# Deferred PSUM copies, a reordered layer norm pipeline, a carried head tail and an early output-weight load in a differential-attention and FFN kernel on eight cores

## The chip, the cores and the metric

The kernel runs on the 8 cores of one Trainium2 chip, with no traffic between them. Core c works on batch element c // 2, and of its 2048 rows on every second block of 128 (8 blocks, 1024 rows). The metric is the device time of the slowest core in microseconds (us), the median over runs.

## The reference, cut to what matters

```python
xn = _layernorm(x)                              # x: (4, 2048, 2048)
s = attn(xn)
g = silu(ffn(xn))
return x + s * g

def attn(x):                                    # 8 heads, two maps of width 128 each
    q1, q2 = split(x @ Wq); k1, k2 = split(x @ Wk)
    vcat = concat(split(x @ Wv))                # width 256
    attn1 = softmax(causal(q1 @ k1.T * scale)) @ vcat
    attn2 = softmax(causal(q2 @ k2.T * scale)) @ vcat
    a = attn1 - lambda_full * attn2
    a = a * rsqrt(mean(a * a) + EPS) * subln_weight * (1.0 - LAMBDA_INIT)
    return heads_joined(a) @ Wo

def ffn(x):                                     # INTER = 5632
    hdn = silu((x @ gate_w.T) * gate_s) * ((x @ up_w.T) * up_s)
    return (hdn @ down_w.T) * down_s
```

## The kernel before

All instruction streams are written out by hand in program order, one list for each engine, and tied by counting semaphores (`wait(engine, semaphore, value)`). Each engine runs its list strictly in order, so the place of an instruction in the emission order decides what stands behind it. Three counters matter: `sT` for TensorE (PE), `sV` for VectorE (DVE), `sS` for ScalarE (ACT). PSUM is split in `psA` and `psB`. The first 1024 columns of `psA` are two slots of 512 that `take_slot` hands out in turn, to projection rounds and to score groups alike; before a slot is written again, PE waits for what emptied it (`slot_guard`).

**Stage 1, layer norm and the projections of head 0 (lines 337 to 480).** A loop over 24 tiles of 128 rows: 16 key/value tiles (all rows of the batch element), then 8 of the core's own rows. For a tile t: `ln_stageA` squares it on ACT (L369) and sums it on DVE (L372); `ln_var` and `ln_rstd` make the inverse deviation (DVE L385 and L389, then Ln and Exp on ACT, L394 and L397); `ln_affine` normalises it on DVE (L404, L408); `ln_tp` transposes it on PE, 16 float32 transposes in four groups (L201, `psB<-ident,xn_nat`), each group copied out by ACT (L434). `h0_rounds` then runs head 0's projection rounds on what is there: a V round for each key/value tile (16 matmuls of 256 columns), two K rounds with every fourth (16 matmuls of 512 columns each), two Q rounds with every fourth own tile. ACT copies each round out right after it (L317, L321, L325). In iteration t the order is rstd(t-1), affine(t-1), transposes(t-1) with their copies, square and sum of t, variance of t, rounds of t-1. The x tiles rotate through three buffers, loaded by the SP queue.

**Stage 2, attention, a loop over 8 heads (lines 483 to 658).** For heads 1 to 7 the 4 Q rounds and the K and V rounds of chunks 0 and 1 (12 rounds) run ahead of the head's tiles; the 12 rounds of chunks 2 and 3 are `pending` and are put one by one between scores and values, one for each map in tiles 0 to 5. DVE copies each round out (L316, L320, L324). For tile tl (0 to 7) and each map beta: score groups of up to 4 blocks, the last group first (PE, then the exponential on ACT, L605; only the last group gets the mask multiply on DVE, L615), a pending round, then the values product into an accumulator that alternates by tl. There are 1 group in tiles 0 and 1, 2 in tiles 2 and 3, 3 in 4 and 5, 4 in 6 and 7. After both maps of tile tl, `emit_combine(tl - 1)` is emitted: ten small DVE steps (L526 to L543), Ln and Exp on ACT (L546, L548), a last DVE step (L553). `emit_atp` transposes its result on PE later (L201, `psB<-ident,a_out`), and ACT copies it (L572). At the end of a head its last combine and transposes are emitted before the next head's Q rounds. GpSimd loads the next head's weights.

**Stage 3, the FFN** in six chunks. The change doesn't touch it. Its result stays in `out_accT` in SBUF.

**Stage 4, gate and output (lines 776 to 865).** 32 groups of 4 transposes of `out_accT` go through two slots of `psB`, each followed by a Silu on ACT into `g_sb` (L795). Then GpSimd loads `wo` into `wo_sb`, four pieces of 2 MB as stored; `wo_sb` lies on the same bytes as `out_accT`, piece i exactly on the four `out_accT` columns blocks of g4 = i. The output product needs all four pieces for its first result; DVE multiplies by the gate and adds x (L851, L853), the SP queue stores.

Of the kernel before, what the change touches and what calls it, by code (L numbers as in the profile page):

```python
# [7 lines left out]
AF = mybir.ActivationFunctionType  # L8
ALU = mybir.AluOpType
AX = mybir.AxisListType.X  # L10
# [27 lines left out]
def build_nc(cfg):  # L38
# [237 lines left out]
    slot_guard = [[], []]  # L276

    def take_slot():
# [6 lines left out]
    def emit_proj_round(h, kind, aa, bb, extra_s_wait=0, evac="vector"):  # L285
# [40 lines left out]
        if evac == "vector":  # L326
            wait("vector", sT, last_c)
            c = sV.bump()
            E("vector", lambda v, fn=fnv, hh=sV.h: fn(v).then_inc(hh, 1))
            slot_guard[i] = [(sV, c)]  # L330
            return (sV, c)
        else:
            wait("scalar", sT, last_c)
            c = sS.bump()
            E("scalar", lambda s, fn=fns, hh=sS.h: fn(s).then_inc(hh, 1))
            slot_guard[i] = [(sS, c)]
            return (sS, c)
# [99 lines left out]

    def h0_rounds(tt):
        ev = sS.n
        if tt < TS:  # L440
            emit_proj_round(0, "v", tt, 0, extra_s_wait=ev, evac="scalar")
            if tt % 4 == 3:
                sc = tt // 4
                emit_proj_round(0, "k", 0, sc, extra_s_wait=ev, evac="scalar")
                emit_proj_round(0, "k", 1, sc, extra_s_wait=ev, evac="scalar")
        else:
            if (tt - TS) % 4 == 3:
                qc = (tt - TS) // 4
                emit_proj_round(0, "q", 0, qc, extra_s_wait=ev, evac="scalar")
                emit_proj_round(0, "q", 1, qc, extra_s_wait=ev, evac="scalar")  # L450

    c_xnT_full = None
    for t in range(NT):
        if t >= 1:
            ln_rstd(t - 1)
            ln_affine(t - 1)
            if t + 2 < NT:
                emit_xdma(t + 2)
            ln_tp(t - 1)
            if t - 1 == TS - 1:  # L460
                c_xnT_full = sS.n
        ln_stageA(t)
        ln_var(t)
        if t >= 1:
            h0_rounds(t - 1)
# [5 lines left out]
    h0_rounds(NT - 1)  # L471
    c_xnT_own = sS.n
# [8 lines left out]

    c_proj_evacs_s0 = sS.n
    for h in range(H):
# [8 lines left out]
        def emit_round(spec):  # L492
            c, kind, aa, bb = spec
            ev = emit_proj_round(h, kind, aa, bb)
            if kind == "v" and aa == 4 * c + 3:
                c_chunk_ev[c] = ev
            return ev

        if h > 0:
            first = True  # L500
            for j in range(2):
                for qc in range(NQC):
                    emit_proj_round(h, "q", j, qc,
                                    extra_s_wait=(c_xnT_own if first else 0))
                    first = False
            for c in range(min(2, NSC)):
                for spec in chunk_rounds(c):
                    emit_round(spec)
            for c in range(2, NSC):
                pending += chunk_rounds(c)  # L510
# [6 lines left out]

        def emit_combine(tl):
            avslot = tl % 2
            avbase = psA[:, 1024:2048] if avslot == 0 else psB[:, 0:1024]  # L520
            av1 = avbase[:, 0:512]
            av2 = avbase[:, 512:1024]
            if h == 0 and tl == 0:
                wait("vector", sLAM, c_lam)
                wait("vector", sV, cv_w2)
            cv = V(lambda v, av1=av1: v.reciprocal(sm_rr1[:, 0:1], av1[:, 256:257]))  # L526
            cv = V(lambda v, av2=av2: v.reciprocal(sm_rr2[:, 0:1], av2[:, 256:257]))
            wait("vector", sV, cv)
            cv = V(lambda v: v.tensor_mul(sm_rr2l[:, 0:1], sm_rr2[:, 0:1],
                                          lamneg[:, 0:1]))  # L530
            wait("vector", sV, cv)
            cv = V(lambda v, av1=av1: v.tensor_scalar(  # L532
                t_comb[:, :], av1[:, 0:256], sm_rr1[:, 0:1], None, ALU.mult))
            wait("vector", sV, cv)
            c_av_free[avslot] = V(lambda v, av2=av2: v.scalar_tensor_tensor(  # L535
                t2buf[:, :], av2[:, 0:256], sm_rr2l[:, 0:1], t_comb[:, :],
                ALU.mult, ALU.add))
            wait("vector", sV, c_av_free[avslot])
            cv = V(lambda v: v.tensor_mul(t_comb[:, :], t2buf[:, :], t2buf[:, :]))  # L539
            wait("vector", sV, cv)  # L540
            cv = V(lambda v: v.reduce_sum(sm_ms[:, 0:1], t_comb[:, :], axis=AX))  # L541
            wait("vector", sV, cv)
            cv_ms = V(lambda v: v.tensor_scalar(  # L543
                sm_ms[:, 0:1], sm_ms[:, 0:1], 1.0 / 256, 1e-5, ALU.mult, ALU.add))
            wait("scalar", sV, cv_ms)
            cs = SC(lambda s: s.activation(sm_rst[:, 0:1], sm_ms[:, 0:1], AF.Ln))  # L546
            wait("scalar", sS, cs)
            c_rstd = SC(lambda s: s.activation(  # L548
                sm_rst[:, 0:1], sm_rst[:, 0:1], AF.Exp, scale=-0.5))
            wait("vector", sS, c_rstd)  # L550
            wait("vector", sT, c_atp_slot[tl % 2])
            ao = a_out[:, (tl % 2) * 256:(tl % 2) * 256 + 256]
            c_aout = V(lambda v, ao=ao: v.scalar_tensor_tensor(  # L553
                ao, t2buf[:, :], sm_rst[:, 0:1], W2[:, :],
                ALU.mult, ALU.mult))
            return c_aout

        def emit_atp(tl, c_aout):
            atp = tl % 2
            ao = a_out[:, atp * 256:atp * 256 + 256]  # L560
            tp = psB[:, 1024 + atp * 512:1024 + atp * 512 + 512]
            wait("tensor", sV, c_aout)
            wait("tensor", sS, c_atp_free[atp])
            for j in range(2):
                TP(tp[:, j * 128:(j + 1) * 128], ao[:, j * 128:(j + 1) * 128],
                   inc=(j == 1))
            c_atp_slot[atp] = sT.n
            wait("scalar", sT, c_atp_slot[atp])
            dst = aT.rearrange("p (at s) -> p at s", s=OWN)[
                :, 2 * h:2 * h + 2, tl * 128:(tl + 1) * 128]  # L570
            c_atp_free[atp] = sS.bump()
            E("scalar", lambda s, dst=dst, tp=tp, hh=sS.h: s.copy(  # L572
                dst, tp.rearrange("p (j c) -> p j c", c=128)[:, 0:2, :]
            ).then_inc(hh, 1))

        pend_atp = []
        for tl in range(TO):
# [4 lines left out]
            while pending and pending[0][0] <= tl // 2:  # L582
                emit_round(pending.pop(0))
# [59 lines left out]
            if len(pend_atp) >= 2:  # L643
                emit_atp(*pend_atp.pop(0))
            if tl > 0:
                ca = emit_combine(tl - 1)
                pend_atp.append((tl - 1, ca))
        if len(pend_atp) >= 2:
            emit_atp(*pend_atp.pop(0))
        ca = emit_combine(TO - 1)  # L650
        pend_atp.append((TO - 1, ca))
        while pend_atp:
            emit_atp(*pend_atp.pop(0))
# [124 lines left out]

    gb_slot_free = [0, 0]
    wait("tensor", sV, c_ffn_done)  # L780
    for tl in range(TO):
        for g4 in range(KD // 4):
            gslot = g4 % 2
# [3 lines left out]
            for kk in range(4):  # L787
# [9 lines left out]
                AF.Silu).then_inc(hh, 1))  # L797
    c_g_done = sS.n

    wo_r = wo.rearrange("(kt p) n -> p kt n", p=128)  # L800
    c_wo = []
    for c4 in range(KD // 4):
        if c4 == 0:
            wait("gpsimd", sS, c_g_done)
        c_wo.append(dma("gpsimd", sWO[c4],
                        wo_sb.rearrange("p (kt n) -> p kt n", n=D)[:, c4 * 4:(c4 + 1) * 4, :],
                        wo_r[:, c4 * 4:(c4 + 1) * 4, :]))
# [182 lines left out]
```

## Time and profile before

| | us |
|---|---|
| median of 3 runs (2566.83, 2572.0, 2770.03) | 2572.0 |
| the profiled execution | 2565.12 |
| its span on the slowest core, core 3 | 2563.6 |
| spans of the eight cores | 2531.9 to 2563.6 |
| PE / DVE / ACT busy on core 3 | 2052.6 / 655.1 / 401.6 |

Three lines of the page show the span of core 3 in 40 equal slices of 64 us, each digit the busy share in tenths (PEclk: the clock granted to TensorE in tenths of full speed):

```profile
PE   2655547879787878787787998998998998999388
ACT  2333333030302121121213000000000000000200
PEclk9766668989998989899899999999999999999689
```

Slices 1 to 6 are stage 1, 7 to 22 attention, 23 to 37 the FFN, the last three stage 4. PE is the engine that is busy most, but not in stage 1 (about 5 tenths, at a clock of 0.6) nor in the third slice from the end. The page's largest waits of PE are these (engine, line, waited for: us in total, times, longest):

```profile
PE psA L194 <- ACT p_buf L605: 148.1, 98, 3.9
PE psB L201 <- DVE xn_nat L408: 123.8, 24, 39.9
PE psA L194 <- ACT xn_nat L369: 48.5, 17, 3.1
PE psA L194 <- DMA wo_sb<-wo: 47.9, 4, 23.1
PE psB L201 <- DVE a_out L553: 29.9, 8, 3.7
```

The first is in attention, the next two in stage 1, the fourth in stage 4, the last at the ends of the heads.

### The profile page before, as it was taken

The numbers are of one execution on the slowest core, as the hardware profiler recorded it, in microseconds if no ns is written. First come the engines' busy times: TensorE is split into PE (matmuls) and PEld (weight loads), VectorE is DVE, ScalarE is ACT, GpSimd is POOL, SyncE is SP. The second block draws the span as 40 slices with busy tenths as digits, with TensorE's granted clock in tenths as the row PEclk, the third lists the DMA queues.
The fourth block names the chain that finished last, engine by engine and source line by source line (L and its number), as shares of the span: only waits on it lengthen the run. The fifth ranks groups of instructions, "written<-read, shape, count | busy, mean of one in ns | idle before, by whom it ended". The sixth has DMA issues, their size and how long they took to land.

```text
span 2563.6 us, 28997 instructions; the slowest of 8 cores (2531.9 to 2563.6 us)
## 1 busy us (share of the span) xinstructions
PE 2052.6 (80%) x11264; PEld 1130.6 (44%) x11264; DVE 655.1 (26%) x1282; ACT 401.6 (16%) x812; POOL 136.3 (5%) x126
## 2 busy tenths in 40 slices
PE   2655547879787878787787998998998998999388
PEld 1433324545555555555455443443443443444234
DVE  2322323232323232333323022021131130123033
ACT  2333333030302121121213000000000000000200
POOL 0000000000000000000000110100101101100000
PEclk9766668989998989899899999999999999999689
DMA  7221231121212112121107956747638729731643
GB/s 135 75 74 66 82 65 18 17 34 17 34 17 34 17 18 33 17 34 17 17 1 87 93 52 84 71 43 99 66 33 114 69 34 107 72 50 17 134 129 132
DMA packets 246058, 147.88 MB, mean 58 GB/s; under 512 B 183587, under 2 KB 232997, under 8 KB 240678
## 3 DMA queue, kind: packets, MB, share of 16 engines
q0 software_dynamic: 239008, 102.77, 34.1%
q1 hardware_dynamic: 6918, 43.25, 4.8%
q8 instruction: 95, 1.56, 0.2%
q14 instruction: 37, 0.30, 0.0%
HBM read 240.38 MB, written 8.39 MB: 97 GB/s over the span
## 4 chain that ended last, share of the span: by engine, by line
PE 74%; DVE 8%; DMA 7%; ACT 6%; issue 5%; DVEq 0%; POOL 0%; ACTq 0%; SPq 0%; POOLq 0%
PE psA L194 52%; PE psB L194 18%; PE psB L201 4%; DMA up_sb<-up_wT 3%; ACT p_buf L605 2%; DMA wo_sb<-wo 2%; ACT xn_nat L369 2%; DVE xn_nat L408 1%; DVE t_comb L532 1%; DVE t2buf L535 1%; DVE t_comb L539 1%; DVE sm_ms L541 1%; DVE vbuf L324 1%; DVE kT L320 1%; ACT sm_rst L546 1%
## 5 line engine op out<-in xcount | busy, mean ns | idle before, releaser
L194 PE MATMUL psA<-wv_sb,xnT_full 128*128 128x256 bf16 x2048 | 282.7, 303 | 77.4 <-ACT xn_nat L369 45.6
L194 PEld LDWEIGHTS psA<-wv_sb,xnT_full 128*128 128x128 bf16 x2048 | 215.4, 107 | 136.3 <-issue 91.6
L194 PE MATMUL psA<-xnT_full,wk_sb 128*128 128x512 bf16 x1024 | 243.3, 396 | 38.0 <-ACT p_buf L605 29.8
L605 ACT ACTIVATE p_buf<-psA 128x512 bf16<-128x512 f32 (+1 forms) x320 | 165.4, 550 | 563.9 <-PE psA L194 555.4
L194 PE MATMUL psA<-xnT_own,gate_sb 128*128 128x512 bf16 x704 | 166.2, 397 | 38.1 <-DMA up_sb<-up_wT 38.1
L201 PE MATMUL psB<-ident,xn_nat 128*128 128x128 f32 x384 | 87.5, 406 | 125.0 <-DVE xn_nat L408 123.8
L194 PE MATMUL psA<-qT,kT 128*128 128x128 bf16 x1152 | 109.3, 229 | 94.9 <-ACT p_buf L605 90.1
L194 PEld LDWEIGHTS psA<-xnT_full,wk_sb 128*128 128x128 bf16 x1024 | 102.0, 101 | 165.5 <-issue 61.7
L194 PE MATMUL psA<-hdn,down_sb 128*128 128x512 bf16 x704 | 159.7, 379 | 11.2 <-DVE hdn L737 11.0
L194 PE MATMUL psB<-hdn,down_sb 128*128 128x512 bf16 x704 | 159.8, 379 | 0.0
L194 PE MATMUL psA<-xnT_own,up_sb 128*128 128x512 bf16 x704 | 155.5, 379 | 0.0
L194 PE MATMUL psB<-xnT_own,gate_sb 128*128 128x512 bf16 x704 | 155.5, 379 | 0.0
L194 PE MATMUL psB<-xnT_own,up_sb 128*128 128x512 bf16 x704 | 155.5, 379 | 0.0
L194 PE MATMUL psA<-wo_sb,aT 128*128 128x512 bf16 x512 | 116.0, 390 | 47.9 <-DMA wo_sb<-wo 47.9
L194 PEld LDWEIGHTS psA<-qT,kT 128*128 128x128 bf16 x1152 | 83.3, 103 | 116.0 <-issue 110.9
L201 PEld LDWEIGHTS psB<-ident,xn_nat 128*128 128x128 f32 x384 | 68.3, 210 | 145.1 <-issue 142.3
L194 PE MATMUL psA<-xnT_own,wq_sb 128*128 128x512 bf16 x512 | 126.2, 412 | 3.9 <-ACT xn_nat L369 2.8
L194 PEld LDWEIGHTS psA<-xnT_own,gate_sb 128*128 128x128 bf16 x704 | 71.0, 101 | 130.5 <-issue 54.9
L727 ACT ACTIVATE silu_g<-psA,gate_sc 128x1024 f32<-128x1024 f32 x22 | 24.5, 1114 | 601.2 <-PE psA L194 601.2
L737 DVE SCALAR_TENSOR_TENSOR hdn<-psA,up_sc,silu_g 128x1024 bf16<-128x1024 f32 x22 | 28.2, 1284 | 328.0 <-PE psA L194 328.0
L194 PEld LDWEIGHTS psA<-hdn,down_sb 128*128 128x128 bf16 x704 | 67.9, 98 | 96.6 <-issue 16.5
L194 PEld LDWEIGHTS psA<-xnT_own,up_sb 128*128 128x128 bf16 x704 | 68.9, 98 | 83.0
(83 smaller groups left out, 1677.6 us busy)
## 6 DMA issues: line engine op xcount, KB each, us to landing
gate_sb<-gate_wT POOLq DMA_DIRECT2D x44, 512.0 KB, 7.7
up_sb<-up_wT POOLq DMA_DIRECT2D x44, 512.0 KB, 9.4
down_sb<-down_wT POOLq DMA_DIRECT2D x5, 4096.0 KB, 30.9
x_stage<-x_kv SPq DMA_DIRECT2D x16, 1024.0 KB, 5.6
wq_sb<-wq POOLq DMA_DIRECT2D x8, 1024.0 KB, 9.4
wk_sb<-wk POOLq DMA_DIRECT2D x8, 1024.0 KB, 9.4
wv_sb<-wv POOLq DMA_DIRECT2D x8, 1024.0 KB, 9.2
x_stage<-x_own SPq DMA_DIRECT2D x8, 1024.0 KB, 4.9
```

Source lines behind the costliest of these rows:

```text
L194: tn.matmul(o, l, r, start=st, stop=sp, skip_group_check=True)))
L201: tn.transpose(o, i_, ident[:, :])))
L320: fnv = lambda e, d=d_, ps=ps: e.tensor_copy(d, ps)
L324: fnv = lambda e, d=d_, ps=ps: e.tensor_copy(d, ps[:, 0:256])
L369: cs_sq[t] = SC(lambda s, xs=xs, xn=xn, t=t: s.activation(xn, xs, AF.Square, accum_out=st_ssq[:, t:t + 1]))
L408: c_ln_aff[t] = V(lambda v, xs=xs, xn=xn, t=t: v.tensor_scalar(xn, xs, st_rstd[:, t:t + 1], st_nmr[:, t:t + 1], ALU.mult, ALU.add))
L532: cv = V(lambda v, av1=av1: v.tensor_scalar(t_comb[:, :], av1[:, 0:256], sm_rr1[:, 0:1], None, ALU.mult))
L535: c_av_free[avslot] = V(lambda v, av2=av2: v.scalar_tensor_tensor(t2buf[:, :], av2[:, 0:256], sm_rr2l[:, 0:1], t_comb[:, :], ALU.mult, ALU ...
L539: cv = V(lambda v: v.tensor_mul(t_comb[:, :], t2buf[:, :], t2buf[:, :]))
L541: cv = V(lambda v: v.reduce_sum(sm_ms[:, 0:1], t_comb[:, :], axis=AX))
L605: s.activation(pb[:, g * 512:g * 512 + w], ps[:, 0:w], AF.Exp).then_inc(hh, 1))
L737: v.scalar_tensor_tensor(hdn[:, itl * OWN:(itl + 1) * OWN], gps[:, OWN:2 * OWN], up_sc[:, it:it + 1], silu_g[:, :], ALU.mult, ALU.mult).th ...
```

## The change

Four edits, all in the order of emission; no instruction is added or taken away.

1. **Stage 1, order.** Square, sum and variance of tile t are emitted ahead of the transposes of tile t-1 and their copies. The rounds of t-1 then wait for those copies and no longer for the square of t.
2. **Deferred copies.** A round's copy out of PSUM is no longer emitted behind its matmuls, but when its slot is next taken (`slot_pending`, `drain_slot` in `take_slot`). This holds for head 0's rounds in stage 1 (on ACT) and for the 12 pending rounds of each later head (on DVE); the 16 rounds ahead of a head's tiles keep their copy behind them (`defer=False`).
3. **Head tail.** The last combine of a head and its outstanding transposes are carried over and emitted after the next head's 16 leading rounds (after the last head, as before). `emit_combine` and `emit_atp` are moved out of the loop unchanged but for a head argument.
4. **Stage 4.** The loop over gate groups runs g4 outside and tl inside, and each piece of `wo` is issued after its g4 is through, instead of all after the last.

```diff
     def take_slot():
         i = PS_["i"]
         PS_["i"] ^= 1
+        drain_slot(i)
         for sem, cnt in slot_guard[i]:
             wait("tensor", sem, cnt)
         return i, psA[:, i * 512:i * 512 + 512]
...
+        if defer:
+            return i, do_evac
+        return do_evac()
...
+    def h0_emit(kind, aa, bb, ev):
+        i, th = emit_proj_round(0, kind, aa, bb, extra_s_wait=ev, evac="scalar",
+                                defer=True)
+        slot_pending[i] = th
...
             ln_affine(t - 1)
             if t + 2 < NT:
                 emit_xdma(t + 2)
+        ln_stageA(t)
+        ln_var(t)
+        if t >= 1:
             ln_tp(t - 1)
             if t - 1 == TS - 1:
                 c_xnT_full = sS.n
-        ln_stageA(t)
-        ln_var(t)
-        if t >= 1:
             h0_rounds(t - 1)
...
+            def fin(th=th, c=c, kind=kind, aa=aa):
+                ev = th()
+                if kind == "v" and aa == 4 * c + 3:
+                    c_chunk_ev[c] = ev
+            if defer:
+                slot_pending[i] = fin
+            else:
+                fin()
...
+        if carry is not None:
+            hp, patp = carry
+            if len(patp) >= 2:
+                emit_atp(hp, *patp.pop(0))
+            ca = emit_combine(hp, TO - 1)
+            patp.append((TO - 1, ca))
+            while patp:
+                emit_atp(hp, *patp.pop(0))
+            carry = None
...
             while pending and pending[0][0] <= tl // 2:
-                emit_round(pending.pop(0))
+                emit_round(pending.pop(0), defer=False)
+            if h > 0 and c_chunk_ev[tl // 2] is None:
+                drain_all_slots()
...
-        if len(pend_atp) >= 2:
-            emit_atp(*pend_atp.pop(0))
-        ca = emit_combine(TO - 1)
-        pend_atp.append((TO - 1, ca))
-        while pend_atp:
-            emit_atp(*pend_atp.pop(0))
+        drain_all_slots()
+        carry = (h, pend_atp)
...
-    for tl in range(TO):
-        for g4 in range(KD // 4):
-            gslot = g4 % 2
+    for g4 in range(KD // 4):
+        for tl in range(TO):
+            gslot = (g4 * TO + tl) % 2
...
+        wait("gpsimd", sS, gb_slot_free[(g4 * TO + TO - 1) % 2])
+        c_wo[g4] = dma("gpsimd", sWO[g4],
+                       wo_sb.rearrange("p (kt n) -> p kt n", n=D)[:, g4 * 4:(g4 + 1) * 4, :],
+                       wo_r[:, g4 * 4:(g4 + 1) * 4, :])
```

## Rows read from the trace of the kernel before

**Rows 1.** Windows by stage, core 3: stretch, length, busy (instructions) by engine, clock, DMA, GB/s

```profile
39.95:276.40 236.45, 143.66 (x640) 94.36 (x641) 69.22 (x113) 83.32 (x152) 0.00 (x0) 0.70 0.20 71
276.40:365.20 88.80, 46.06 (x193) 29.30 (x194) 30.24 (x50) 36.97 (x64) 0.43 (x1) 0.65 0.17 60
435.90:1394.17 958.27, 764.75 (x5266) 501.51 (x5264) 296.84 (x812) 182.09 (x448) 26.00 (x23) 0.92 0.19 24
2369.30:2393.80 24.50, 19.62 (x128) 13.41 (x128) 0.14 (x1) 18.92 (x32) 0.00 (x0) 1.00 0.00 1
2393.80:2446.50 52.70, 5.61 (x13) 1.35 (x14) 0.00 (x0) 0.00 (x0) 2.98 (x4) 0.53 0.97 199
```

**Rows 2.** Timeline of one key/value tile: start, us, engine, work, [idle before <-releaser]

```profile
183.42 3.85 PE L201 MATMUL psB<-ident,xn_nat 128*128 128x128 f32 x16 [3.03 <-DVE xn_nat L408]
...
187.84 1.91 ACT L369 ACTIVATE xn_nat<-x_stage 128x2048 f32<-128x2048 f32 x1
...
190.09 3.57 PE L194 MATMUL psA<-wv_sb,xnT_full 128*128 128x256 bf16 x16 [2.83 <-ACT xn_nat L369]
...
194.03 0.21 ACT L394 ACTIVATE st_rstd<-st_t 128x1 f32<-128x1 f32 x1
...
194.90 1.35 DVE L408 TENSOR_SCALAR xn_nat<-x_stage,st_rstd,st_nmr 128x2048 f32<-128x2048 f32 x1
...
196.50 3.85 PE L201 MATMUL psB<-ident,xn_nat 128*128 128x128 f32 x16 [2.84 <-DVE xn_nat L408]
```

**Rows 3.** Timeline: two K rounds, an own tile, an own tile with Q rounds

```profile
206.54 8.13 PE L194 MATMUL psA<-xnT_full,wk_sb 128*128 128x512 bf16 x32
...
295.14 3.85 PE L201 MATMUL psB<-ident,xn_nat 128*128 128x128 f32 x16 [5.73 <-DVE xn_nat L408]
...
304.72 3.47 PE L201 MATMUL psB<-ident,xn_nat 128*128 128x128 f32 x16 [5.73 <-DVE xn_nat L408]
...
322.84 1.06 PE L201 MATMUL psB<-ident,xn_nat 128*128 128x128 f32 x8 [3.05 <-DVE xn_nat L408]
323.56 1.07 ACT L434 CAST xnT_own<-psB 128x512 bf16<-128x512 f32 x2 [2.69 <-PE psB L201]
```

**Rows 4.** Windows of 4 us in head 0's attention, columns as in rows 1

```profile
396.00:400.00 4.00, 2.95 (x16) 2.20 (x16) 2.61 (x10) 1.25 (x6) 0.00 (x0) 0.52 0.00 2
...
404.00:408.00 4.00, 2.09 (x23) 1.68 (x23) 2.45 (x7) 2.02 (x6) 0.00 (x0) 1.00 0.00 0
```

**Rows 5.** Timeline of tiles 1 and 2 of a head with pending rounds

```profile
763.20 0.69 DVE L320 CAST kT<-psA 128x512 bf16<-128x512 f32 x1 [3.46 <-PE psA L194]
...
766.05 0.42 DVE L324 CAST vbuf<-psA 128x256 bf16<-128x256 f32 x1 [1.29 <-PE psA L194]
766.22 0.39 PE L194 MATMUL psA<-qT,kT 128*128 128x128 bf16 x4
766.62 1.91 PE L194 MATMUL psA<-wv_sb,xnT_full 128*128 128x256 bf16 x16
766.70 0.60 ACT L605 ACTIVATE p_buf<-psA 128x512 bf16<-128x512 f32 x1 [2.48 <-PE psA L194]
767.40 0.42 DVE L615 TENSOR_TENSOR p_buf<-p_buf,masks 128x512 bf16<-128x512 bf16 x1 [0.93 <-ACT p_buf L605]
...
768.97 0.16 DVE L526 RECIPROCAL sm_rr<-psA 128x1 f32<-128x1 f32 x1
...
772.05 0.20 ACT L546 ACTIVATE sm_rst<-sm_ms 128x1 f32<-128x1 f32 x1 [4.75 <-DVE sm_ms L543]
...
772.97 3.57 PE L194 MATMUL psA<-wv_sb,xnT_full 128*128 128x256 bf16 x16 [3.38 <-ACT p_buf L605]
```

**Rows 6.** Timeline of the end of a head and the next head's start

```profile
839.18 2.03 PE L194 MATMUL psB<-vbuf,p_buf 128*128 128x257 bf16 x16
...
847.39 0.66 PE L201 MATMUL psB<-ident,a_out 128*128 128x128 f32 x2 [3.74 <-DVE a_out L553]
847.84 2.72 PE L194 MATMUL psA<-xnT_own,wq_sb 128*128 128x512 bf16 x6
```

More of the change, by code:

```diff
@@ L276, in build_nc, with drain_slot, drain_all_slots @@
     slot_guard = [[], []]
+    slot_pending = [None, None]
+    def drain_slot(i):
+        if slot_pending[i] is not None:
+            th = slot_pending[i]
+            slot_pending[i] = None
+            th()
+    def drain_all_slots():
+        drain_slot(0)
+        drain_slot(1)
     def take_slot():
@@ L325, in emit_proj_round, with do_evac @@
             fns = lambda e, d=d_, ps=ps: e.copy(d, ps[:, 0:256])
[L326 to L337, printed above, removed]
+        def do_evac():
+            if evac == "vector":
+                wait("vector", sT, last_c)
+                c = sV.bump()
+                E("vector", lambda v, fn=fnv, hh=sV.h: fn(v).then_inc(hh, 1))
+                slot_guard[i] = [(sV, c)]
+                return (sV, c)
+            else:
+                wait("scalar", sT, last_c)
+                c = sS.bump()
+                E("scalar", lambda s, fn=fns, hh=sS.h: fn(s).then_inc(hh, 1))
+                slot_guard[i] = [(sS, c)]
+                return (sS, c)
+        if defer:
+            return i, do_evac
+        return do_evac()
     NT = TS + TO
@@ L448, in h0_rounds @@
                 qc = (tt - TS) // 4
[L449 to L450 removed]
+                h0_emit("q", 0, qc, ev)
+                h0_emit("q", 1, qc, ev)
     c_xnT_full = None
@@ L480, in build_nc, with emit_combine @@
         vones.rearrange("p (t c) -> p t c", c=1)).then_inc(hh, 1))
+    def emit_combine(h, tl):
+        avslot = tl % 2
+        avbase = psA[:, 1024:2048] if avslot == 0 else psB[:, 0:1024]
+        av1 = avbase[:, 0:512]
+        av2 = avbase[:, 512:1024]
+        if h == 0 and tl == 0:
+            wait("vector", sLAM, c_lam)
+            wait("vector", sV, cv_w2)
+        cv = V(lambda v, av1=av1: v.reciprocal(sm_rr1[:, 0:1], av1[:, 256:257]))
+        cv = V(lambda v, av2=av2: v.reciprocal(sm_rr2[:, 0:1], av2[:, 256:257]))
+        wait("vector", sV, cv)
+        cv = V(lambda v: v.tensor_mul(sm_rr2l[:, 0:1], sm_rr2[:, 0:1],
+                                      lamneg[:, 0:1]))
+        wait("vector", sV, cv)
+        cv = V(lambda v, av1=av1: v.tensor_scalar(
+            t_comb[:, :], av1[:, 0:256], sm_rr1[:, 0:1], None, ALU.mult))
+        wait("vector", sV, cv)
+        c_av_free[avslot] = V(lambda v, av2=av2: v.scalar_tensor_tensor(
+            t2buf[:, :], av2[:, 0:256], sm_rr2l[:, 0:1], t_comb[:, :],
+            ALU.mult, ALU.add))
+        wait("vector", sV, c_av_free[avslot])
+        cv = V(lambda v: v.tensor_mul(t_comb[:, :], t2buf[:, :], t2buf[:, :]))
+        wait("vector", sV, cv)
+        cv = V(lambda v: v.reduce_sum(sm_ms[:, 0:1], t_comb[:, :], axis=AX))
+        wait("vector", sV, cv)
+        cv_ms = V(lambda v: v.tensor_scalar(
+            sm_ms[:, 0:1], sm_ms[:, 0:1], 1.0 / 256, 1e-5, ALU.mult, ALU.add))
+        wait("scalar", sV, cv_ms)
+        cs = SC(lambda s: s.activation(sm_rst[:, 0:1], sm_ms[:, 0:1], AF.Ln))
+        wait("scalar", sS, cs)
+        c_rstd = SC(lambda s: s.activation(
+            sm_rst[:, 0:1], sm_rst[:, 0:1], AF.Exp, scale=-0.5))
+        wait("vector", sS, c_rstd)
+        wait("vector", sT, c_atp_slot[tl % 2])
+        ao = a_out[:, (tl % 2) * 256:(tl % 2) * 256 + 256]
+        c_aout = V(lambda v, ao=ao: v.scalar_tensor_tensor(
+            ao, t2buf[:, :], sm_rst[:, 0:1], W2[:, :],
+            ALU.mult, ALU.mult))
+        return c_aout
@@ new lines, in emit_atp @@
+    def emit_atp(h, tl, c_aout):
+        atp = tl % 2
+        ao = a_out[:, atp * 256:atp * 256 + 256]
+        tp = psB[:, 1024 + atp * 512:1024 + atp * 512 + 512]
+        wait("tensor", sV, c_aout)
+        wait("tensor", sS, c_atp_free[atp])
+        for j in range(2):
+            TP(tp[:, j * 128:(j + 1) * 128], ao[:, j * 128:(j + 1) * 128],
+               inc=(j == 1))
+        c_atp_slot[atp] = sT.n
+        wait("scalar", sT, c_atp_slot[atp])
+        dst = aT.rearrange("p (at s) -> p at s", s=OWN)[
+            :, 2 * h:2 * h + 2, tl * 128:(tl + 1) * 128]
+        c_atp_free[atp] = sS.bump()
+        E("scalar", lambda s, dst=dst, tp=tp, hh=sS.h: s.copy(
+            dst, tp.rearrange("p (j c) -> p j c", c=128)[:, 0:2, :]
+        ).then_inc(hh, 1))
@@ L490, in chunk_rounds, with emit_round @@
             return r
-        def emit_round(spec):
+        def emit_round(spec, defer=True):
             c, kind, aa, bb = spec
[L494 to L497, printed above, removed]
+            i, th = emit_proj_round(h, kind, aa, bb, defer=True)
+            def fin(th=th, c=c, kind=kind, aa=aa):
[4 more added lines that the diff above has]
+                slot_pending[i] = fin
+            else:
+                fin()
         if h > 0:
@@ L516, in build_nc @@
         w_prefetched = False
[L518 to L574, printed above, removed]
+        if carry is not None:
[6 more added lines that the diff above has]
+                emit_atp(hp, *patp.pop(0))
+            carry = None
```

33 lines of the change are left out of this document (18 added, 15 removed).

## The prediction

> **What bounds the kernel now.** I read the spans and clocks of the cores first (undisturbed, all at about 0.90), then the page's slices, then windows cut at the stage borders, then the list of waits to see which stage each big wait of PE lies in, and last the timeline of one unit of each stage that the diff touches. The windows [rows 1] say where there is anything to win. The 16 key/value tiles of stage 1 take 236.45 us with PE busy for 143.66 at a granted clock of 0.70; the 8 own tiles 88.80 with PE busy for 46.06. The seven heads with pending rounds take 958.27 at 0.92, 136.9 each. The gate transposes take 24.50, and the load of `wo` behind them 52.70, with PE nearly idle and the DMA engines at 0.97. The FFN, untouched, is dense.
>
> No engine bounds stage 1; a chain does. In one tile [rows 2] the reader sees it walk over three engines: transposes at 183.42, the square of the next tile at 187.84 behind the last copy, the V round at 190.09, which waited 2.83 for that square, Ln at 194.03 behind the round's copy, the affine at 194.90, next transposes at 196.50. That is 13.08 us for 7.4 us of matmuls, and PE idles twice for 2.8 us.
>
> **Edit 1 and 2 in stage 1.** The square (1.91 on ACT) now runs beside the affine and the first transposes, and Ln(t) no longer stands behind the copy of V round t-1, but behind that of a round two takes older, done long before. The cycle left is: transposes and their four copies, 4.42 (187.84 - 183.42); then the old copy, about 0.3; then two branches in parallel. On PE the V round starts at about 4.9 and keeps PE 3.4 (3.57 less the drain of the last matmul). On ACT and DVE, Ln to next transposes is 2.47 (196.50 - 194.03), ready at 7.2. PE is last: 8.3 us a tile at the low clock of 1.2 GHz, in place of 13.08. Every fourth tile adds two K rounds, 8.13 [rows 3]: they now run on behind the V round, with the affine hidden under them. Four tiles: 4 x 8.3 + 8.1 = 41.3, all 16: 165, a gain of 71.
>
> At 2.4 GHz the transposes are copy-bound: 8 of them in 1.06, two copies in 1.07 from 0.72 after the start [rows 3]; with two slots the four copies end at about 3.1. Add 0.3 and 2.47: 5.9 a tile, the ACT and DVE branch being last (the V round, 1.91 [rows 5], ends at 5.5). K rounds are four times a V round's column work, 7.0, of which 6.6 shows. Four tiles 30.2, all 121, a gain of 115.
>
> Which clock? Before, it is mostly low, and each tile has idle gaps of 2.8 and 3.0 us. Afterwards the longest gap I can construct is 1.2 to 1.3 us (last transpose to V round), and at the low clock PE would be busy 7 of 8.3 us. In head 0's attention the clock rose from 0.52 to 1.00 around a stretch busy 2.95 of 4.00, and stayed at 1.00 in one busy 2.09 of 4.00 [rows 4], close to the 3.5 of 5.9 I expect here at the high level. So I take three quarters of the stage at the high level: 132 us, a gain of 104. Range 71 to 115.
>
> The Trainium skill (TensorE: Matmul & The Clock Gate, Part 4: PE-mode transpose) says the full clock doesn't engage for transposes, which don't count as busy in the same way; half of PE's work here is transposes. By that the gain would be the 71 of the low level. The trace speaks against it: 24.50 us of nothing but such transposes ran at 1.00 [rows 1]. It shows the level being held, not reached, so the low case stays a rival.
>
> Own tiles: 9.58 (5.73 + 3.85 [rows 3]) becomes 4.42 + 2.47 = 6.9 since the square leaves the chain; six of them save 16. The tile with Q rounds took 18.12 (304.72 to 322.84); now 4.9 + 8.7 = 13.6, saving 4.5. Together 21. The last tile keeps its chain. The x loads are issued by SP behind the same affine as before and are needed two periods later, 12 us at the least; the DMA share of 0.20 would at most double. DVE has 4.3 us of work in a tile (69.22 over 16), ACT 5.2 (83.32 over 16) [rows 1], both under 5.9.
>
> **Edit 2 in attention.** This one costs. Drained at the next take of its slot, a pending round's copy goes into DVE's list behind the mask of the score group emitted just before, and PE's very next take waits for it. In rows 5: round r3 starts at 766.62, 0.40 after its scores (766.22), since the previous copy (766.05) was long in. Now DVE would do the mask first: exponential 766.70 to 767.30, mask 767.40 to 767.82, copy 0.42, so r3 at 768.4: +1.8. Behind PE's wait stand the round and the values product; nothing else can run. A head has seven such places (second map of tile 0, both of tile 1, second maps of 2 to 5). With a narrow exponential, or where the round waited for an exponential anyway, it is 1.0 to 1.1; with a K copy (0.69 [rows 5]) or a third group 1.5. Sum of the seven: 10.1; bounds 7 and 12.6.
>
> The other five places, the first maps of tiles 2 to 6, gain. There the combine of an earlier tile stood on DVE behind the copy of the round just finished (it starts at 768.97), its Ln came 3.08 later, and the exponentials of the next tile stood behind that Ln on ACT, so PE waited 3.38 for r4. Now the combine starts as r3 starts, 2.3 us earlier against r3, but scores' second group then waits for exponential, L553, mask and copy. From r3 to r4 I get 5.3 in place of 6.35 (772.97 - 766.62). The five give 0.6 to 1.45 each, 4.9 in all; bounds 3 and 7. Net +5.2 a head, +36 for seven; bounds 0 and +67.
>
> **Edit 3.** Before, PE has nothing from the end of the last values product (841.2) to the first Q round (847.84) but four transposes: 6.6 us [rows 6]. The carried combine is emitted after the sixteen rounds with DVE's copies ahead of it, and the transposes that need it still stand ahead of the next scores on PE. So the stall isn't hidden, it moves: copy 0.42, combine 4.2 (3.08 to Ln [rows 5], Ln, Exp and L553), transposes 0.6: 5.2. What is gained is the end of the combine before it, 1.4 a head, 10 in all. Bounds: nothing, and 2.5 a head.
>
> **Edit 4.** Piece 0 is issued a quarter into the 24.50 us, 18.4 earlier. The pieces are issued every 6.1 us while one takes 13.2 of the 52.70, so the chain of four slides by the full 18.4; the x loads are issued as before and share the engines as before. Below bound 12, if the new order slows transposes or copies.
>
> **Sum**, against the profiled execution's own 2565.1: -104 - 21 + 36 - 10 - 18 = -117, which gives 2448. The median of the runs shown is 7 us above it, the lowest 2 above; I leave the forecast at 2448. About 2% (51 us) is what a measurement of this kernel can tell from no change.
>
> **Rivals.** (a) *Stage 1 stays at 1.2 GHz*, by the rule on transposes or because short gaps are enough: +33, 2481. The mean clock of the stage decides, which before is 0.70. 17%. (b) *The deferred copies cost their upper bound*, 9.6 a head in place of 5.2: +31, 2479. For it: the waits of PE for DVE and ACT in series at every slot; against: all durations are from rows. 12%. (c) *Slower, by the clock in attention.* The new 1.5 to 2 us stalls come between those of 2.5 to 3 us that stay, and the heads run at 0.92 on the strength of their density. If the twelve rounds, scores and values of the loop (an estimate of 51 us of matmul time a head at the full clock: 8 V rounds at 1.75, 4 K rounds at 3.5, and 144 blocks at 0.11 for values and 0.055 for scores, scaled by columns from r3's 1.91 [rows 5]) went to the low level, the price would be up to 45 a head, 315 in all, 2763. It cancels the gain from 17 us a head, when over a third of this work runs low. Against it: rows 4, where stalls of the same kind leave the clock at 1.00. 4% for slower by over 2%, 5% for a part of it that ends within 2%. (d) *The reverse*: shorter longest stalls keep the heads at the high level where they now fall (r4 takes 3.57 at 772.97 where r3 took 1.91): -3 a head, 2425. 12%. The forecast itself has 50%.
>
> The range takes in (a), (b), (d) and the high bound of stage 1: 2405 to 2500, with some 10% on either side, more above. Faster by over 2% means under 2521: 0.91 (the forecast, a, b and d); same 0.05; slower 0.04.
>
> **What would show it.** Right: first Q round of head 1 some 125 us earlier; tiles of about 6 us with the V round released by an ACT copy and clock near 1.0 up to the own tiles, where it falls; in the heads, PE waiting 1 to 2 us for DVE copies (L320, L324) inside tiles, and for L553 in front of a head's first scores rather than its Q rounds; heads of about 140 us; `wo` waits of about 30. Wrong: a clock under 0.7 in stage 1, tiles of 8 us or more, heads over 150 or under 136.

## The result: 4.9% faster

| | before | after |
|---|---|---|
| median of 10 runs | 2653.63 us | 2443.87 us |
| lowest | 2566.83 us | 2437.53 us |
| profiled execution, its span | 2565.12, 2563.6 us | 2437.53, 2436.0 us |
| ratio, 95% interval | | 0.9507 [0.9491, 0.9523] |

Five of the ten runs of before and three of the ten of the changed kernel fell in a slower state that this chip shows in some executions of any kernel, which lifts the medians; the ratio and all times below leave such runs out (2567 to 2572 is left, against 2438 to 2450). The forecast was 2448 and a ratio of 0.952.

The windows of the changed kernel, cut at the same borders as [rows 1] (core 1, its slowest; length, busy time and instructions of PE, PEld, DVE, ACT, POOL, granted clock, DMA share, GB/s): key/value tiles, own tiles, heads 1 to 7, gate transposes, the wait for `wo`.

```profile
40.60:167.00 126.40, 98.01 (x654) 68.22 (x655) 71.82 (x117) 78.86 (x152) 0.00 (x0) 1.00 0.44 142
167.00:230.40 63.40, 41.17 (x180) 26.38 (x179) 27.63 (x45) 33.94 (x62) 0.40 (x1) 0.73 0.21 67
...
293.60:1284.20 990.60, 759.09 (x5273) 499.67 (x5271) 293.65 (x824) 183.79 (x455) 26.00 (x23) 0.93 0.18 23
...
2258.30:2282.40 24.10, 19.61 (x128) 13.39 (x128) 0.00 (x0) 18.90 (x32) 2.23 (x3) 1.00 0.63 103
2282.40:2319.10 36.70, 4.76 (x13) 1.23 (x14) 0.00 (x0) 0.03 (x1) 0.74 (x1) 0.55 1.00 219
```

Against [rows 1], the 236.45 us of the key/value tiles became 126.40, and the clock 1.00 in place of 0.70; the own tiles went from 88.80 to 63.40; the seven heads from 958.27 to 990.60, longer; the wait for `wo` from 52.70 to 36.70. By stage, on the slowest core of each kernel (stage 1 from the first transpose to the first score, attention from there to the first gate matmul, the FFN from there to the first gate transpose): stage 1 325.3 to 189.8, attention 1028.9 to 1053.8, FFN 975.5 to 974.1, everything after the gate transposes 170.9 to 154.5. That is -135.5, +24.9, -1.4 and -16.4; with a first transpose 0.7 us later, it gives the 127.6 between the spans.

One key/value tile of the changed kernel (timeline, columns as in [rows 2]):

```profile
58.65 0.22 ACT L410 ACTIVATE st_rstd<-st_t 128x1 f32<-128x1 f32 x1
58.90 1.91 PE L194 MATMUL psA<-wv_sb,xnT_full 128*128 128x256 bf16 x16 [1.39 <-ACT st_rstd L410]
...
59.06 1.90 ACT L385 ACTIVATE xn_nat<-x_stage 128x2048 f32<-128x2048 f32 x1
...
59.52 1.35 DVE L424 TENSOR_SCALAR xn_nat<-x_stage,st_rstd,st_nmr 128x2048 f32<-128x2048 f32 x1
...
61.13 1.06 PE L201 MATMUL psB<-ident,xn_nat 128*128 128x128 f32 x8 [0.32 <-ACT xn_nat L385]
...
62.58 1.12 PE L201 MATMUL psB<-ident,xn_nat 128*128 128x128 f32 x8 [0.39 <-ACT xnT_full L450]
...
64.79 1.91 PE L194 MATMUL psA<-wv_sb,xnT_full 128*128 128x256 bf16 x16 [1.10 <-ACT vbuf L337]
```

From V round to V round it is 5.89 us where [rows 2] has 13.08. Ln starts before the V round and no longer behind its copy; the square and the affine run beside the round; PE's gaps are 1.10, 0.32 and 0.39, and its matmuls run at nearly twice the speed of [rows 2] (1.91 for the V round against 3.57).

### The profile page after: what moved, and what is told of

It is laid out like the page before. It is cut to its first block, busy times and chain, and to the rows that moved or that the text cites. A ratio compares the mean times of both kernels' runs of the same rounds, so it can differ in the third digit from the quotient of the medians.

```text
span 2436.0 us, 29000 instructions; the slowest of 8 cores (2387.9 to 2436.0 us)
## 1 busy us (share of the span) xinstructions
PE 1997.2 (82%) x11264; PEld 1100.3 (45%) x11264; DVE 648.4 (27%) x1282; ACT 396.2 (16%) x812; POOL 136.3 (6%) x126
## 4 chain that ended last, share of the span: by engine, by line
PE 74%; DVE 7%; DMA 6%; ACT 6%; issue 5%; DVEq 0%; ACTq 0%; POOL 0%; SPq 0%; POOLq 0%
PE psA L194 52%; PE psB L194 19%; DMA up_sb<-up_wT 3%; ACT p_buf L646 3%; PE psB L201 3%; DMA wo_sb<-wo 1%; DVE vbuf L336 1%; DVE kT L332 1%; DVE st_sum L388 1%; ACT xn_nat L385 1%; DVE t_comb L518 1%; DVE t2buf L521 1%; DMA x_stage<-x_kv 1%; DVE a_out L539 1%; DVE p_buf L656 1%
## 5 line engine op out<-in xcount | busy, mean ns | idle before, releaser
L194 PE MATMUL psA<-wv_sb,xnT_full 128*128 128x256 bf16 x2048 | 267.3, 293 | 60.8 <-ACT p_buf L646 16.5
L194 PEld LDWEIGHTS psA<-wv_sb,xnT_full 128*128 128x128 bf16 x2048 | 208.9, 104 | 108.9 <-issue 71.0
L194 PE MATMUL psA<-xnT_full,wk_sb 128*128 128x512 bf16 x1024 | 248.4, 402 | 11.4 <-DVE kT L332 11.4
L656 DVE TENSOR_TENSOR p_buf<-p_buf,masks 128x512 bf16<-128x512 bf16 (+1 forms) x128 | 45.8, 358 | 367.8 <-ACT p_buf L646 362.1
L201 PE MATMUL psB<-ident,xn_nat 128*128 128x128 f32 x384 | 64.2, 321 | 69.0 <-DVE xn_nat L424 44.2
L194 PE MATMUL psA<-xnT_own,wq_sb 128*128 128x512 bf16 x512 | 114.0, 384 | 2.6 <-ACT qT L329 1.3
L194 PEld LDWEIGHTS psB<-xnT_own,up_sb 128*128 128x128 bf16 x704 | 68.9, 98 | 83.0
```

Source lines behind the costliest of these rows:

```text
L194: tn.matmul(o, l, r, start=st, stop=sp, skip_group_check=True)))
L201: tn.transpose(o, i_, ident[:, :])))
L656: v.tensor_mul(pb[:, g * 512:g * 512 + w], pb[:, g * 512:g * 512 + w], masks[:, tl * 512:tl * 512 + w]).then_inc(hh, 1))
```

## The experiments

Four kernels make one part of the change each, on the kernel before, with what the part needs of `slot_pending` and its draining. The stage lengths are medians of the eight cores of the profiled execution; for the kernel before they are 324.6 (stage 1), 1026.0 (attention) and 171.0 (after the gate transposes), for the changed kernel 189.4, 1048.8 and 152.2.

| kernel | stage 1 | attention | after the gate | time |
|---|---|---|---|---|
| stage 1 alone | 188.9 | 1025.7 | 170.9 | 2438 to 2452, ratio 0.9477 [0.9413, 0.954] |
| deferred copies in the heads alone | 323.8 | 1067.6 | 171.1 | 2614 to 2630, ratio 1.0165 [1.0108, 1.0223] |
| carried tail alone | 322.9 | 1016.0 | 170.7 | 2570.69, one |
| early `wo` alone | 325.1 | 1025.8 | 154.2 | 2559 to 2573, ratio 0.9935 [0.9896, 0.9975] |

### Stage 1 alone

```diff
+        ln_stageA(t)                     # ahead of ln_tp(t - 1)
+        ln_var(t)
...
+        slot_pending[i] = th             # head 0's copies, drained at the next take
```

> The kernel before with edits 1 and 2 in stage 1 alone; copies in the heads, head tail and wo load as before. Theory (stage 1 is a chain over three engines, and its parts add to the others): stage 1 takes 190 us in place of 325, key/value tiles at a clock of 1.00; total 135 lower, about 2434 against 2569 for the kernel before. Rival (the copies left behind their rounds in the heads, or the later start of the weight loads, take some of it back): a gain under 120, above 2449.

Stage 1 is 135.7 us shorter and nothing else moved, 1025.7 in attention against 1026.0. The theory holds: this part alone gives as much as the whole change, 2438 to 2452 against 2438 to 2450, and by stages somewhat more, 135.7 us against the 127.6 between the spans.

### Deferred copies in the heads alone

```diff
-                    emit_round(pending.pop(0))
+                    emit_round(pending.pop(0), defer=True)
```

> The kernel before with only the copies of the 12 pending rounds of each later head deferred. Theory of the prediction: seven places lose 10.1 us, five gain 4.9, net +5.2 a head, +36 in all, about 2605. Rival A (the carried head tail really hides its stall, and the deferral costs all of what the tail gave): attention as a whole came out 25 longer, so the deferral would be +65, 2634. Rival B (the clock in the heads falls with the added stalls): over +60 with a mean clock in the heads under 0.90. Rival C (the deferral is free, and the tail costs the 25): 2569.

Attention is 41.6 us longer, 5.9 a head where 5.2 was forecast, so rivals A (65) and C (nothing) fall. Over heads 1 to 7 the granted clock was 0.926 to 0.930 by core, against 0.916 to 0.918 for the kernel before: it didn't fall, and rival B falls too.

### The carried tail alone

```diff
+        carry = (h, pend_atp)            # combine and transposes after the next 16 rounds
```

> The kernel before with only the last combine and transposes of a head carried behind the next head's sixteen leading rounds. Theory: the stall of about 5 us is moved in front of the next head's first scores and only the end of the combine before it is won, 1.4 to 2.5 us a head, 10 to 17 in all, 2552 to 2559. Rival (the stall is hidden): 5 us or more a head, 35 to 45 in all, 2524 to 2534. Rival (it costs, since the clock falls in front of the scores and a K round in place of the Q rounds): 2575 or more.

Attention is 10.0 us shorter, the lower end of the theory, and no more. The total can't decide here: there is one time to compare, 2570.69, and the kernel before, run beside it, took 2572 to 2598. The length of attention does, 1012.5 to 1019.3 by core against 1026.0 to 1029.5.

### The early load of `wo` alone

```diff
-    for tl in range(TO):
-        for g4 in range(KD // 4):
+    for g4 in range(KD // 4):
+        for tl in range(TO):
...
+        c_wo[g4] = dma("gpsimd", sWO[g4], ...)    # after each g4
```

> The kernel before with only the order of the gate groups turned and each piece of wo issued after its quarter. Theory: 16 us less, as between the two traces (52.7 to 36.7 from the last gate transpose to the last wait for wo), 2553. Rival (the earlier pieces only crowd the x loads and the first stores): under 8, 2561 or more.

The part after the gate transposes is 16.8 us shorter, as in the changed kernel. The waits of its output product (timeline of the changed kernel) are 15.03, 7.70 and 8.93 where the kernel before had four, 47.9 in all:

```profile
2298.73 1.87 PE L194 MATMUL psA<-wo_sb,aT 128*128 128x512 bf16 x4 [15.03 <-DMA wo_sb<-wo]
2308.30 1.86 PE L194 MATMUL psA<-wo_sb,aT 128*128 128x512 bf16 x4 [7.70 <-DMA wo_sb<-wo]
2319.09 11.16 PE L194 MATMUL psA<-wo_sb,aT 128*128 128x512 bf16 x41 [8.93 <-DMA wo_sb<-wo]
```

The DMA engines were at 0.63 over the gate transposes and at 1.00 in the 36.70 us behind them: the load is still bound by the transfer, it only starts earlier.

### Each half of the edit in stage 1

The first keeps each copy behind its round and only moves square, sum and variance up; the second only defers the copies.

```diff
+        ln_stageA(t)                     # first kernel
+        ln_var(t)
```

> The kernel before with the square, sum and variance ahead of the transposes in stage 1, but each copy still behind its round. Theory: the square leaves the chain, Ln still stands behind the copy of the V round; a key/value tile is transposes and copies 4.4, V round 3.5, copy 0.4, Ln to transposes 2.5, 10.8 us in place of 13.1 at the low clock; own tiles 6.9 as with both. Gain 16 x 2.3 + 8 x 2.7 = 55 to 60, 2512. If the clock rises as it did with both, tiles of 8.0 and a gain near 100, 2470. Rival (either half alone does it all): 2434.

```diff
+        slot_pending[i] = th             # second kernel
```

> The kernel before with the copies of head 0's rounds deferred in stage 1, but the square still between the transposes' copies and the rounds. Theory: Ln no longer waits for the V round, but the round waits for the square; a key/value tile is transposes and copies 4.4, square 2.1 and its latency, V round 3.4, 10.2 us in place of 13.1 at the low clock; own tiles keep their 9.6 since the square stays in their chain, but for the one with Q rounds (-3). Gain 16 x 2.9 + 3 = 45 to 50, 2521. If the clock rises, tiles of 8.4 and a gain near 80, 2489. Rival (the two edits are additive and this one holds the larger part): 80 or more at a clock as before.

Only stage 1 is read from these two. It took 263.4 and 263.0 (medians, all cores within 261.4 to 264.4): 61 us less for either half, 123 for the two added up, 135.7 together. Both were forecast low, at 55 to 60 and 45 to 50. Their timelines on PE, the order alone first, then the deferral alone:

```profile
183.44 3.39 PE L208 MATMUL psB<-ident,xn_nat 128*128 128x128 f32 x16 [3.05 <-ACT xn_nat L392]
187.75 3.39 PE L201 MATMUL psA<-wv_sb,xnT_full 128*128 128x256 bf16 x16 [0.93 <-ACT xnT_full L457]
193.98 3.62 PE L208 MATMUL psB<-ident,xn_nat 128*128 128x128 f32 x16 [2.83 <-ACT xn_nat L392]
```

```profile
181.59 3.36 PE L208 MATMUL psB<-ident,xn_nat 128*128 128x128 f32 x16
188.15 3.57 PE L201 MATMUL psA<-wv_sb,xnT_full 128*128 128x256 bf16 x16 [3.20 <-ACT kT L340]
191.52 3.36 PE L208 MATMUL psB<-ident,xn_nat 128*128 128x128 f32 x16
```

Each half closes one of the two gaps of [rows 2] and leaves the other: 0.93 and 2.83 in the first, none and 3.20 in the second. The tiles shown take 10.5 and 9.9 us. With one gap of 3 us left, the granted clock over the key/value tiles was 0.77 to 0.81 on all cores; with none it was 1.00. Some 13 us of the 135.7 exist only with both halves, 10 of them in the key/value tiles (43 and 55 less for the halves, 108 together, medians from the first transpose to the end of the last K round). That the clock accounts for them is likely, but no run separates it from the chain.

### Transposes twice, a question on the clock

```diff
-            for kt in kts:
+            for kt in (kts * 2 if t >= TS else kts):     # own tiles only
                 TP(ps[...], xn[:, kt * 128:(kt + 1) * 128], ...)
```

> The changed kernel with each transpose of the 8 own tiles of stage 1 issued twice, same result; a question on the clock alone. In the changed kernel these tiles hold only transposes and idle gaps of 3.0 us and run at 0.50 but for what the K and Q rounds leave behind. Theory (transposes are activity as any matmul): with nearly no gaps the clock goes from 0.50 to 1.00 inside the own tiles and stays there, and the stage gets little longer although its transposes are doubled, 63 to at most 70 us. Rival, by the Trainium skill (TensorE: Matmul & The Clock Gate, Part 4: PE-mode transpose), where the full clock doesn't engage for transposes: 0.50 throughout, tiles of about 10.3 us (transposes 6.9 + the rest of 3.5), the stage near 90.

In the changed kernel the own tiles hold one idle gap of 3.04 us each. Between the K rounds and the Q rounds they run at the low clock (16 transposes in 3.85):

```profile
170.47 3.85 PE L201 MATMUL psB<-ident,xn_nat 128*128 128x128 f32 x16 [3.04 <-ACT xn_nat L385]
177.35 3.85 PE L201 MATMUL psB<-ident,xn_nat 128*128 128x128 f32 x16 [3.04 <-ACT xn_nat L385]
```

Behind the first Q rounds the level went to and fro on core 1 (on core 6 it stayed low), and rose there too after a stretch of nothing but transposes:

```profile
203.80:207.20 3.40, 3.27 (x15) 2.82 (x16) 2.70 (x5) 1.41 (x4) 0.00 (x0) 0.50 0.00 0
207.20:210.60 3.40, 0.36 (x3) 0.15 (x2) 1.75 (x3) 3.18 (x6) 0.00 (x0) 1.00 0.00 0
```

With each transpose doubled, on core 0, first two tiles of the timeline, then windows of 4 us around them:

```profile
203.85 5.35 PE L208 MATMUL psB<-ident,xn_nat 128*128 128x128 f32 x32 [3.04 <-ACT xn_nat L392]
212.25 3.83 PE L208 MATMUL psB<-ident,xn_nat 128*128 128x128 f32 x32 [3.04 <-ACT xn_nat L392]
```

```profile
204.00:208.00 4.00, 4.00 (x23) 4.00 (x23) 2.42 (x5) 1.17 (x2) 0.00 (x0) 0.57 0.00 0
208.00:212.00 4.00, 1.20 (x12) 0.96 (x9) 1.51 (x3) 3.20 (x6) 0.00 (x0) 1.00 0.00 0
212.00:216.00 4.00, 3.75 (x32) 3.46 (x32) 2.82 (x5) 1.92 (x5) 0.00 (x0) 1.00 0.00 0
```

The clock went from 1.2 to 2.4 GHz inside a stretch that holds nothing but transposes, and 32 then took what 16 had taken. The rule of the Trainium skill that I weighed in the prediction (TensorE: Matmul & The Clock Gate, Part 4: PE-mode transpose) doesn't hold for these float32 transposes. My expectation was right in kind and too strong in degree. The gap of 3.04 us remains in every tile, and the level isn't held on all cores: stage 1 took 191.7 us on the best core and 204.9 on the worst, against a median of 189.4 in the changed kernel. The two worst, cores 6 and 7, also show a third figure, a granted clock of 0.81, as from 201.6 to 208.4 on core 6, where cores 1, 3 and 4 show 1.00, so their times say less of the transposes.

### The changed kernel without the deferral in the heads

```diff
-                    emit_round(pending.pop(0))
+                    emit_round(pending.pop(0), defer=False)
```

> The changed kernel with the copies of the pending rounds in heads 1 to 7 put back behind their rounds; all else as changed. Theory: the deferral there costs 36, so 2441 - 36 = 2405. Rival (the deferral pays for itself with the carried tail, whose combine would otherwise collide): 2441 or more. Rival A of the heads-only run: 2376.

Attention 1015.6, 33.2 less than in the changed kernel; the times are 2408 to 2418 against 2438 to 2450. Edit 2 in the heads is a net loss, and the change would have been worth 30 us more without it. What the deferral does is seen in the changed kernel's tile 1 (core 1):

```profile
352.09 0.60 ACT L646 ACTIVATE p_buf<-psA 128x512 bf16<-128x512 f32 x1 [5.29 <-PE psA L194]
352.79 0.43 DVE L656 TENSOR_TENSOR p_buf<-p_buf,masks 128x512 bf16<-128x512 bf16 x1 [5.00 <-ACT p_buf L646]
353.13 0.68 DVE L332 CAST kT<-psA 128x512 bf16<-128x512 f32 x1
353.96 1.91 PE L194 MATMUL psA<-wv_sb,xnT_full 128*128 128x256 bf16 x16 [1.97 <-DVE kT L332]
...
357.67 0.42 DVE L336 CAST vbuf<-psA 128x256 bf16<-128x256 f32 x1
358.00 0.16 DVE L512 RECIPROCAL sm_rr<-psA 128x1 f32<-128x1 f32 x1
...
358.23 1.91 PE L194 MATMUL psA<-wv_sb,xnT_full 128*128 128x256 bf16 x16 [1.70 <-DVE sm_rr L513]
...
362.35 0.42 DVE L336 CAST vbuf<-psA 128x256 bf16<-128x256 f32 x1
...
362.91 0.38 PE L194 MATMUL psA<-qT,kT 128*128 128x128 bf16 x4 [2.22 <-DVE vbuf L336]
363.13 2.56 PE L194 MATMUL psA<-wv_sb,xnT_full 128*128 128x256 bf16 x16
```

Exponential, mask, copy, round stand one behind the other, and PE waits 1.97 and 1.70 where [rows 5] shows the round r3 starting 0.40 after its scores (the twelve rounds of a head are counted from r0, so r3 is that of the second map of tile 1, and r4 that of the first map of tile 2). (The 1.70 is put down to L513, the instruction behind the copy on DVE; what PE needs is the copy at 357.67.) The gain stands beside it: the combine begins at 358.00, with the round, and from round to round it is 4.90 (358.23 to 363.13) in place of 6.35 in [rows 5].

### A split tail: the combine at the head's end, its transposes carried

```diff
         drain_all_slots()
+        if len(pend_atp) >= 2:
+            emit_atp(h, *pend_atp.pop(0))
+        ca = emit_combine(h, TO - 1)
+        pend_atp.append((TO - 1, ca))
         carry = (h, pend_atp)            # only transposes are carried
```

> The changed kernel without the deferral in the heads, and with the head tail split: the last combine is emitted at the end of its own head, as in the kernel before, and only the transposes that need it are carried behind the next head's sixteen rounds. Theory (in the changed kernel the stall is moved, not hidden, because the combine went with the transposes): the stall of 5.2 us goes, attention is 1015.5 - 7 x 5.2 = 979 us on a core of the shorter kind, total about 2405 - 36 = 2370. Rival (DVE's copies of the Q rounds then stand behind the combine and stall PE there): attention over 1000, less than half of it won. Rival (the gap in front of the scores let the weights land or held something else): 1015.

This is made on the kernel of the last section, with no copy deferred in the heads. Attention 968.3, 47.3 less than without the split; the times are 2360.63 and 2361.81. The changed kernel's head start (core 1) and this one's (core 3):

```profile
335.21 0.60 PE L201 MATMUL psB<-ident,a_out 128*128 128x128 f32 x4
340.33 0.66 PE L201 MATMUL psB<-ident,a_out 128*128 128x128 f32 x2 [4.53 <-DVE a_out L539]
...
341.00 4.98 PE L194 MATMUL psA<-xnT_full,wk_sb 128*128 128x512 bf16 x16
```

```profile
715.51 0.60 PE L208 MATMUL psB<-ident,a_out 128*128 128x128 f32 x4
715.95 0.28 PE L201 MATMUL psA<-qT,kT 128*128 128x128 bf16 x2
716.35 3.61 PE L201 MATMUL psA<-xnT_full,wk_sb 128*128 128x512 bf16 x16
```

In the first, PE goes idle for 4.53 us in front of the last two transposes and the K round after that takes 4.98 for 16 matmuls; in the second there is no wait and the K round takes 3.61. The carried tail had moved the stall from the end of a head to the start of the next; only the split hides it. It is worth 6.8 us a head and not 5.2, since the stall also left the clock low behind it (0.50 from 341 to 343): 1.4 of the K round here, and 1.1 to 2.5 over the seven heads of that core, where this kernel's K round takes 3.61 at 1.00 in each.

### Which copies the deferral hurts

Three kernels on the split tail: the copy deferred only in the five places where a combine is emitted between round and copy; only in the other seven; in all twelve.

```diff
+                    emit_round(pending.pop(0), defer=(beta == 1 and tl > 0))        # five
+                    emit_round(pending.pop(0), defer=not (beta == 1 and tl > 0))    # seven
```

> The same as the split tail, but with the copy deferred for the rounds of second maps from tile 1 on, the five places of a head where a combine is emitted between round and copy. Theory: those five gain 4.9 us a head by the prediction's terms and the losing seven are absent, attention 979 - 34 = 945, total about 2336. By the measured sums (deferral alone +6.6 a head, +4.9 on top of the carried tail, where +5.2 was expected) the gain may be smaller: 955. Rival (deferral costs wherever it is used, since the copy stands behind the mask): attention 985 or more.

> The split tail with the copies deferred only in the seven places of a head that the prediction called losing (first maps of tiles 0 to 5, second map of tile 0); the other five copies stand behind their rounds. To be read in the length of attention, 968 us (median of the cores) with no deferral and 950.5 with the other five. Theory of the prediction: +10.1 us a head, 1039. From the measured sums: the deferral as a whole cost 4.5 a head on top of the carried tail and 6 alone, and the five gaining places give 2.5 in place of 4.9, so the seven would cost 7 to 8.5, 1017 to 1028. Rival (the exponential and the mask are mostly hidden by the rounds there): under 1000.

> The split tail with all twelve copies of a head deferred, as in the changed kernel. To be read in the length of attention. If the two kinds of places are independent, it is 968 - 17.5 + what the run with the other places adds. With +5.2 a head as predicted: 1004; with +6 as measured alone on the kernel before: 1010.

| copies deferred | attention, median | against none | time |
|---|---|---|---|
| none | 968.3 | | 2360.63, 2361.81 |
| the five | 950.4 | -17.9 | 2337.18 to 2339.79 |
| the seven | 1039.9 | +71.6 | 2444.82, one |
| all twelve | 998.8 | +30.5 | 2408.67, one |

The seven cost 10.2 us a head; the prediction's term was 10.1. The five give 2.6 a head alone, half of its 4.9, but 5.9 on top of the seven (1039.9 - 998.8). The two kinds of places aren't independent, and the first round of tile 2 shows why. With no copy deferred, round r3 to r4 (timeline on PE, split tail):

```profile
728.05 1.91 PE L201 MATMUL psA<-wv_sb,xnT_full 128*128 128x256 bf16 x16
...
734.39 3.57 PE L201 MATMUL psA<-wv_sb,xnT_full 128*128 128x256 bf16 x16 [3.38 <-ACT p_buf L662]
```

and with the five deferred:

```profile
720.63 1.91 PE L201 MATMUL psA<-wv_sb,xnT_full 128*128 128x256 bf16 x16
...
726.67 0.58 PE L201 MATMUL psA<-qT,kT 128*128 128x128 bf16 x4 [3.58 <-DVE vbuf L343]
727.05 3.39 PE L201 MATMUL psA<-wv_sb,xnT_full 128*128 128x256 bf16 x16
```

6.34 and 6.42: nothing won there. The combine starts behind the mask of the second map, with the five deferred at

```profile
721.76 0.16 DVE L527 RECIPROCAL sm_rr<-psA 128x1 f32<-128x1 f32 x1
```

Where the round isn't held up by a copy, it starts before that mask is done (720.63), so the combine is 1.13 late against it; where it is held up by mask and copy, as in the changed kernel, the combine starts together with it (358.00 and 358.23), and the 4.90 appears. Over all seven heads of all eight cores, r3 to r4 took 6.36 with none deferred, 6.31 with the five, 6.57 with the seven and 5.05 with all twelve. Part of the five's gain is time that the seven had lost.

What this leaves open is the clock. Its median over heads 1 to 7 was 0.935 with none, 0.947 with the five, 0.933 with the seven and 0.955 with all twelve, so some of the 17.9, and of the 5.9 a head, may be clock and not waits; no run separates the two. The rows with the seven and with all twelve rest on one execution each.

The kernel with the five deferred is the fastest found: 2337.18 to 2339.79, a ratio of 0.9093 [0.907, 0.9117] to the kernel before.

## Which steps of the prediction held, and which failed

The total came out near the forecast, but two terms behind it did not: the largest was too small, and one was wrong in kind.

- **Stage 1 is a chain, and both edits break it.** The mechanism was right: the tile of 5.9 us at 2.4 GHz was met at 5.89, the own tiles' 6.9 at 6.88 (170.47 to 177.35). The step that failed is the size of this term, through the clock: -104 - 21 = -125 was forecast, -135.5 measured. I took three quarters of the key/value tiles at the high level, 132 us, a choice between two bounds; all of them ran at 1.00 and took 126.4, a gain of 110 in place of 104. The own tiles, for which I took the low level throughout, gained 25 in place of 21, since behind K and Q rounds their transposes were still at the high level: the first took 5.58 (164.89 to 170.47) and not 6.88. Rival (a) fell.
- **Deferred copies in the heads.** +36 was forecast, +33.2 measured on the carried tail, +41.6 alone, +30.5 on the split one; why it costs least there isn't shown. The losing places were put at 10.1 a head and cost 10.2. The gaining term is the step that was wrong in kind: 4.9 a head was forecast, bounds 3 and 7, and the five places gave 2.6 alone and 5.9 on top of the seven. I had worked it out from a round already delayed by mask and copy and then let it stand as if independent. That the sum didn't suffer is luck of the case: in this change all twelve are deferred together. Rival (b) fell, its 67 is over every figure.
- **The carried tail moves the stall.** Right, -10 forecast and measured. The stall itself, put at 5.2, leaves out what the clock costs behind it: hidden, it gave 6.8.
- **The early `wo`.** -18.4 forecast, -16.4 to -16.8 measured. The chain of four pieces didn't slide quite as a block.
- **The clock in the heads**, rivals (c) and (d). It didn't fall, so (c) is out; over heads 1 to 7 it rose a little, to between 0.924 and 0.933 by core from 0.916 to 0.918. That is the way of (d), but attention came out within 2 us of the sum without it (+24.9 against +26), so (d) isn't borne out as a gain of its own. Its 2425 should have read 2427, 7 x 3 below 2448.
- **The sum.** -117 forecast, -127.6 between the spans. Nearly all of the difference is stage 1, 10.5; attention, the FFN and the end are each within 2 us of their terms.

## What to carry to other kernels

Where three engines hand a tile round in a ring, look for each thing that stands in front of the next stage only by its place in an engine's list, and take all of them out: the two halves here gave 61 each, and together 136. Deferring a copy helps where something needed sooner stands behind it and nothing waits for the slot; where the next instruction but one takes the slot again, the copy ends up behind the mask and the exponential in front of it, and costs their length. A stall that is moved isn't hidden: split the work at the engine border, and carry only the part whose result is needed late.

## What the runs showed of the hardware

- Float32 transposes alone brought TensorE's clock from 0.57 in one window of 4 us to 1.00 in the next. That the gate transposes held it at 1.00 was in [rows 1]; that they reach it was new.
- At one and the same idle gap of 3.04 us a tile, the own tiles with 16 transposes between gaps ran at the low level behind the K rounds and went to and fro behind the Q rounds; with 32 they ran mostly at the high one on core 0, but not on core 6 of the same execution. What decides between cores isn't settled.
- The FFN, the same instructions in every kernel, took from 943 to 999 us by core and execution, more than the tail or the `wo` edit is worth. Such edits were to be read in their own stage and not in the total.
